# Half-precision softmax split: the low half's subtraction moved from two engines to one

## Chip, cores and metric

One core of one Trainium2 chip runs the whole kernel. The metric is the device time of one execution in microseconds (us). The kernel before takes 1481.31 us, the median of three runs (1479.34 to 1484.07). What a measurement of it can tell from no change is about 0.3%, or 4.4 us.

## What is computed

The reference adds three blocks to an input of 16 sequences x 256 tokens x 128 features:

```
x = x + 0.5 * ffn(layernorm(x))     # soft phase 0
x = x + linear_attention(layernorm(x))
x = x + 0.5 * ffn(layernorm(x))     # soft phase 2
# ffn: h = LN(x); x += softmax_attention(h)   (16 heads of 8, causal)
#      h = LN(x); x += mixture of 8 experts, top 2, silu(h w1) * (h w2) w3
# attention: attn = softmax(mask(q k^T) / sqrt(8)); ctx = attn v; ctx wo + bo
```

The change touches only the softmax attention, which runs twice (phases 0 and 2, "soft"). Both of its runs are called softmax cores here.

## The kernel before

**Batches and groups.** A softmax core goes over B = 16 sequences b, and in each over S = 4 groups g of GH = 4 heads. It runs from about 96 to 425 us and again from about 974 to 1300 us of the span. In front of each stands a stage that makes q, k, v; behind each stands the stage of the experts (39 tiles). The linear attention lies between.

**The probabilities in two halves.** With the causal mask, a group has three blocks of 128 x 128 per head, so a tile of 128 partitions x 3 x 4 x 128 = 1536 columns. ScalarE writes exp() into `pf` in f32 (L613) and casts it into `p_hi` in f16 (L630). Then p_lo = pf - p_hi is taken, also in f16. `pf`, `p_hi` and `p_lo` are double buffered by g % 2. TensorE multiplies p_hi and p_lo with the values (L429, function `values`), and sums both in f32. VectorE subtracts the first two blocks (1024 columns, L933 in `p_low` of the vector block) and GpSimd the third (512 columns, L1315 in `p_low` of the gpsimd block). Each has a semaphore, `p_lo_in` and `p_lo2_in`. Two places wait for both: `values` on TensorE and `exps` on ScalarE, which must not overwrite `pf` of two groups ago.

**VectorE's order** is written out in `iteration` (L1019). In step g of sequence b it does `maxima` of the next group (L920, two of the blocks, then L924, the third, both read PSUM), then something of an earlier sequence, then `p_low` of the group before:

- g = 0: `back_add(b-2)` (L969 to L975), `p_low(b-1, 3)`, `place_of(b-3)` (L1011, L1013)
- g = 1: `x_step(b-2)` (L981, x_all = 0.5 y2 + x_all, two f32 inputs in SBUF), `p_low(b, 0)`
- g = 2: `back_context(b-1)` (L946, L948, L953: cx = num * rden, two f32 inputs in SBUF), `p_low(b, 1)`
- g = 3: `choose(b-2)` (L991 to L1004: top 2 experts; L993 a subtraction of two SBUF inputs, L997 and L998 small casts), `p_low(b, 2)`

**GpSimd's order** is written out in `iteration` (L1319):

- g = 0: `p_low(b-1, 3)`, `back_rstd(b-2)` (L1291 to L1294, waits for VectorE's L975), `scatter(b-4, 3)`
- g = 1: `p_low(b, 0)`, `slots(b-3)` (L1250, three of L1253, L1255, each waiting for the one before), `scatter(b-3, 0)`
- g = 2: `p_low(b, 1)`, `scatter(b-3, 1)`
- g = 3: `p_low(b, 2)`, `scatter(b-3, 2)`

A scatter (L1265) is an indirect DMA that GpSimd issues, 128 rows of the normalized tokens to their expert's place. From sequence 4 on all of this is there ("steady" below); in sequences 0 to 3 the parts of earlier sequences are partly missing. Behind the last sequence the chain of `back_rstd`, `choose`, `slots` and scatters goes on alone (the tail) and ends with the load of the first expert tile.

**TensorE's order** in step g: `natural(g+1)` (scores for the maxima, L379, L383), `turned(g)` (transposed scores with mask and minus the maximum, L403 to L410), `values` of two groups before, and at g = 3 `back_turn(b-1)` (L331, needs cx) and `back_wo(b-1)` (L337, L340). SyncE loads `qst` and `kst` of the next sequence in two halves, each once `turned` has read the old one (L1433).

Of the kernel before, what the change touches and what calls it, by code (L numbers as in the profile page):

```python
# [16 lines left out]
ALU = mybir.AluOpType  # L17
# [3 lines left out]
P = 128  # L21
B = 16
# [5 lines left out]
S = G  # L28
GH = H // G
# [39 lines left out]
def build(nc, x, Wq, Wk, Wv, Wo, ln1_s, ln1_b, wq, wk, wv, wo, bo, ln2_s, ln2_b, gate_w, w1, w2, w3, out):  # L69
    ctx = ExitStack()  # L70

    def sb(name, shape, dt=F32):
        return ctx.enter_context(nc.sbuf_tensor(name, shape, dt))

    with ctx:
# [64 lines left out]
        pf = sb("pf", [P, 2, 3, GH, P])  # L140
        p_hi = sb("p_hi", [P, 2, 3, GH, P], F16)
        p_lo = sb("p_lo", [P, 2, 3, GH, P], F16)
# [16 lines left out]
        def parts_of(ph, g):  # L159

            if ph["soft"] or g < 2:
                return p_hi[:, g % 2, :, :, :], p_lo[:, g % 2, :, :, :]
            return more[:, g - 2, :, :, :], more[:, g, :, :, :]
# [37 lines left out]
        def sem(name):  # L201
            return ctx.enter_context(nc.semaphore(name))

        x_in, w_in, consts, outs, passed = [sem("tokens_in_0"), sem("tokens_in_1")], sem("w_in"), sem("consts"), sem("outs"), sem("passed")
# [7 lines left out]
        shared = sems("all", "xn_in hi_in v_hi ht_in v_done qk_done v_out turn_done cx_in pv_out spread_done act_spread "  # L212
                             "dve_spread turned exped p_hi_in p_lo_in pv_done")
        both = "filled emptied stats rstd cv_back cp_front qk_out "
        of_soft = both + "y_in scored negm_in stats2 rstd2 n2_in cp_back x_in p_lo2_in "
        of_soft += "cv_route cv_place n2_kept top_in chosen_in ranked cp_slot scattered"
        of_linear = both + "neg_in exp_in full_in"
        phases = [dict(shared, n=n, soft=soft, w=0 if soft else 1, back_links=4 if soft else 2,
# [31 lines left out]
        def _(pe):  # L250
# [164 lines left out]
            def values(ph, b, g):  # L415

                pe.wait_ge(ph["v_loaded"][g // 2], ph["n"] * (16 * B) + 16 * (b + 1))
                pe.wait_ge(ph["p_lo_in"], ph["n"] * (S * B) + b * S + g + 1)
                if ph["soft"]:
                    pe.wait_ge(ph["p_lo2_in"], b * S + g + 1)  # L420
                if g % 2 == 0 and not (isinstance(b, int) and b == 0 and g == 0):
                    pe.wait_ge(ph["pv_out"], ph["n"] * (2 * B) + 2 * b + g // 2)
                for j in range(GH):
                    h = GH * g + j
                    for tq, blocks in enumerate((((0, 0),), ((0, 2), (1, 1)))):
                        o = (tq * (H // 2) + h % (H // 2)) * VC
                        todo = [(src, tk, c) for tk, c in blocks for src in parts_of(ph, g)]
                        for i, (src, tk, c) in enumerate(todo):
                            ins = nc.tensor.matmul(bank_pv[:, o:o + VC], src[:, c, j, :],  # L429
                                                   v_hl[:, tk, h, :], start=(i == 0), stop=(i == len(todo) - 1),  # L430
                                                   skip_group_check=True)
                ins.then_inc(ph["pv_done"], 1)
# [122 lines left out]
        def _(sc):  # L555
# [49 lines left out]
            def exps(ph, b, g):  # L605

                sc.wait_ge(ph["turned"], ph["n"] * (S * B) + b * S + g + 1)
                flat = "p a b c -> p (a b c)"
                if ph["soft"]:
                    if not (isinstance(b, int) and b == 0 and g < 2):  # L610
                        sc.wait_ge(ph["p_lo_in"], ph["n"] * (S * B) + b * S + g - 1)
                        sc.wait_ge(ph["p_lo2_in"], b * S + g - 1)
                    nc.scalar.activation(pf[:, g % 2, :, :, :].rearrange(flat),  # L613
                                         banks_t[:, :, :].rearrange("p a b -> p (a b)"), ACT.Exp,
                                         scale=HD ** -0.5).then_inc(ph["exped"], 1)
                else:
                    if not (isinstance(b, int) and b == 0):
                        sc.wait_ge(ph["pv_done"], ph["n"] * (S * B) + b * S + g + 1 - 4)
                    nc.scalar.copy(parts_of(ph, g)[0].rearrange(flat),
                                   (banks_t if g % 2 else banks_n)[:, :, :].rearrange("p a b -> p (a b)"))\  # L620
                        .then_inc(ph["p_hi_in"], 1)
# [155 lines left out]
        def _(ve):  # L777
# [149 lines left out]
            def p_low(ph, b, g):  # L927
                ve.wait_ge(ph["p_hi_in"], ph["n"] * (S * B) + b * S + g + 1)
                flat = "p a b c -> p (a b c)"
                hi, lo = [a.rearrange(flat) for a in parts_of(ph, g)]  # L930
                if ph["soft"]:
                    two = slice(0, 2 * GH * P)
                    nc.vector.tensor_tensor(lo[:, two], pf[:, g % 2, :, :, :].rearrange(flat)[:, two], hi[:, two],  # L933
                                            ALU.subtract)\
                        .then_inc(ph["p_lo_in"], 1)
                else:
                    nc.vector.tensor_tensor(lo, (banks_t if g % 2 else banks_n)[:, :, :].rearrange("p a b -> p (a b)"),  # L937
                                            hi, ALU.subtract)\
                        .then_inc(ph["exped"], 1)
# [241 lines left out]
        def _(gp):  # L1181
            pools = sem("pools")
            c = Chain(gp, pools, 0)
# [124 lines left out]
                select(hi)  # L1308
                select(lo).then_inc(ph["p_lo_in"], 1)

            def p_low(ph, b, g):

                gp.wait_ge(ph["p_hi_in"], ph["n"] * (S * B) + b * S + g + 1)
                flat = "p b c -> p (b c)"
                nc.gpsimd.tensor_tensor(p_lo[:, g % 2, 2, :, :].rearrange(flat), pf[:, g % 2, 2, :, :].rearrange(flat),  # L1315
                                        p_hi[:, g % 2, 2, :, :].rearrange(flat), ALU.subtract)\
                    .then_inc(ph["p_lo2_in"], 1)

            def iteration(ph, b, place=4):  # L1319
                for g in range(S):  # L1320
                    causal(ph, b, g)
                    if ph["soft"] and g:
                        p_low(ph, b, g - 1)
                    elif ph["soft"] and place > 0:
                        p_low(ph, b - 1, S - 1)
                    if ph["soft"] and g == 0 and place > 1:
                        back_rstd(ph, b - 2)
                    if ph["soft"] and g == 1 and place > 2:
                        slots(ph, b - 3)
                    if ph["soft"] and g == 0 and place > 3:  # L1330
                        scatter(ph, b - 4, 3)
                    if ph["soft"] and g and place > 2:
                        scatter(ph, b - 3, g - 1)
# [13 lines left out]
            def attention(ph):  # L1347
                if ph["soft"]:
                    front_rstd(ph, 0)
                    if ph is phases[0]:  # L1350
                        front_constants()
                    front_rstd(ph, 1)
                    front_rstd(ph, 2)
                else:
                    for pair in range(PAIRS):
                        front_rstd(ph, pair)
                if ph is phases[0]:
                    core_constants()
                    split_weights()
                    nc.gpsimd.iota(n2_all[:, :, P], pattern=[[2 * P, NT]], base=0, channel_multiplier=2,  # L1360
                                   allow_small_or_imprecise_dtypes=True)
                    nc.gpsimd.iota(beyond[:, :, :], pattern=[[TS, NTI], [P, 2]], base=2 * CAP, channel_multiplier=1,
                                   allow_small_or_imprecise_dtypes=True)
                    nc.gpsimd.iota(iota_h[:, :], pattern=[[P, 2]], base=0, channel_multiplier=1,
                                   allow_small_or_imprecise_dtypes=True).then_inc(consts, 1)
                    gp.wait_ge(w_in, weights_in)
                if ph["soft"]:
                    for b in range(B):
                        iteration(ph, b, place=b)
                    back_rstd(ph, B - 2)  # L1370
                    scatter(ph, B - 4, 3)
                    p_low(ph, B - 1, S - 1)
                    slots(ph, B - 3)
                    for n in range(4):
                        scatter(ph, B - 3, n)
                    back_rstd(ph, B - 1)
                    slots(ph, B - 2)
                    for n in range(4):
                        scatter(ph, B - 2, n)
                    slots(ph, B - 1)  # L1380
                    for n in range(4):
                        scatter(ph, B - 1, n)
                else:
                    with gp.Fori(0, B) as b:
                        iteration(ph, b)
# [150 lines left out]
```

## Time and profile before

| | |
|---|---|
| median of three runs | 1481.31 us (1479.34 to 1484.07) |
| the profiled execution: own time / span | 1481.91 / 1479.9 us |
| VectorE (DVE) busy | 1181.4 us, 80% |
| TensorE (PE) busy | 1097.4 us, 74% |
| ScalarE (ACT) busy | 857.6 us, 58% |
| GpSimd (POOL) busy | 803.9 us, 54% |
| L933, DVE, 128x1024, x128 | 159.3 us, 1245 ns each |
| L1315, POOL, 128x512, x128 | 169.3 us, 1323 ns each |
| L981, DVE, 128x256, x32 | 44.9 + 8.6 us |
| mean granted TensorE clock | 0.874 |

Busy times are sums of instruction durations, and a duration runs from the start to the end of one instruction as recorded. An instruction that is held up inside (by a resource and not by a semaphore) shows this as a longer duration. Instructions of one engine overlap a little: L933 lasts 1.22 us, and the next one starts 1.13 to 1.14 us behind its start. An idle time in brackets is one ahead of the instruction, with what ended it.

### The profile page before, as it was taken

How to read it: one execution, taken by the hardware profiler on the slowest of the kernel's cores; microseconds unless marked ns; L12 is line 12 of the kernel's file. 1: busy time of each engine (PE TensorE's matmuls, PEld its weight loads, DVE VectorE, ACT ScalarE, POOL GpSimd, SP SyncE). 2: the span in 40 equal slices, each digit the busy share in tenths (PEclk: the TensorE clock that was granted, in tenths of full speed). 3: DMA queues.
4: the chain of work that ended last, by engine and by line, in shares of the span. 5: the costliest groups of instructions: out<-in, count | busy, mean ns of one | idle time of the engine just before them, and what ended most of it. 6: DMA issues, size and time to landing. Idle time of an engine off the chain costs nothing.

```text
span 1479.9 us, 38139 instructions
## 1 busy us (share of the span) xinstructions
PE 1097.4 (74%) x12590; PEld 822.3 (56%) x12716; DVE 1181.4 (80%) x2394; ACT 857.6 (58%) x1263; POOL 803.9 (54%) x934
## 2 busy tenths in 40 slices
PE   5778878887837994677666664988888888639980
PEld 4656766666625663554443443866666666526660
DVE  6867999999956885887778776878999999748885
ACT  3556877777724553446555552767777777625550
POOL 6533666666663665112666664124666667646661
PEclk9999999999958998887666665999999999959995
DMA  8911111111102332110111110001111111013326
GB/s 296 403 28 37 45 45 46 45 46 48 42 24 74 90 90 79 49 40 15 52 52 53 54 47 1 18 18 37 50 50 44 46 47 48 28 47 85 90 73 183
DMA packets 124875, 98.64 MB, mean 67 GB/s; under 512 B 41584, under 2 KB 116848, under 8 KB 124784
## 3 DMA queue, kind: packets, MB, share of 16 engines
q1 hardware_dynamic: 115696, 78.71, 18.1%
q0 software_dynamic: 9088, 18.76, 3.9%
q8 instruction: 52, 0.85, 0.2%
q14 instruction: 39, 0.32, 0.1%
HBM read 24.61 MB, written 40.94 MB: 44 GB/s over the span
## 4 chain that ended last, share of the span: by engine, by line
DVE 37%; PE 20%; issue 20%; ACT 8%; POOL 6%; DMA 4%; SPq 3%; DVEq 1%; ACTq 0%; POOLq 0%
DVE negm L920 5%; DVE p_lo L933 4%; POOL ys L1341 4%; DVE negm L924 3%; PE banks_t L403 3%; PE banks_n L278 3%; PE banks_t L296 2%; DVE p_lo L1132 2%; ACT pf L741 2%; SPq L1433 2%; DVE x_all L882 2%; DVE pf L1139 2%; DMA kst<-k_all 2%; DVE cx L953 2%; PE banks_t L410 2%
## 5 line engine op out<-in xcount | busy, mean ns | idle before, releaser
L1315 POOL TENSOR_TENSOR p_lo<-pf,p_hi 128x512 f16<-128x512 f32 x128 | 169.3, 1323 | 192.7 <-ACT p_hi L630 191.0
L613 ACT ACTIVATE pf<-banks_t 128x1536 f32<-128x1536 f32 x128 | 185.7, 1451 | 119.5 <-PE banks_t L410 112.4
L1341 POOL DMA_INDIRECT ys<-q_all,dest x156 | 151.0, 968 | 116.3 <-ACT q_all L747 91.3
L403 PE MATMUL banks_t<-qst,kst 128*128 128x512 f16 x480 | 192.4, 426 | 3.7 <-ACT pf L613 2.1
L630 ACT CAST p_hi<-pf 128x1536 f16<-128x1536 f32 x128 | 188.7, 1474 | 1.1
L920 DVE TENSOR_REDUCE negm<-banks_n 128x4 f16<-128x1024 f32 x128 | 155.9, 1218 | 30.4 <-PE banks_n L383 22.5
L410 PEld LDWEIGHTS banks_t<-ident,negm 128*128 128x128 f16 x1536 | 123.2, 101 | 82.8 <-issue 12.9
L933 DVE TENSOR_TENSOR p_lo<-pf,p_hi 128x1024 f16<-128x1024 f32 x128 | 159.3, 1245 | 4.3 <-ACT p_hi L630 4.2
L1265 POOL DMA_INDIRECT xs<-n_all,slot x128 | 132.7, 1037 | 47.7 <-issue 30.3
L410 PE MATMUL banks_t<-ident,negm 128*128 128x128 f16 x1536 | 154.3, 225 | 0.4 <-issue 0.4
L383 PE MATMUL banks_n<-kst,qst 128*128 128x128 f16 x1536 | 127.8, 219 | 35.3 <-DMA kst<-k_all 16.5
L429 PE MATMUL bank_pv<-v_hl,p_hi 128*128 128x17 f16 x1920 | 118.8, 172 | 23.2 <-POOL p_lo L1301 17.9
L429 PEld LDWEIGHTS bank_pv<-v_hl,p_hi 128*128 128x128 f16 x1920 | 110.9, 98 | 41.7 <-issue 41.6
L383 PEld LDWEIGHTS banks_n<-kst,qst 128*128 128x128 f16 x1536 | 107.3, 98 | 30.8 <-issue 0.3
L429 PE MATMUL bank_pv<-v_hl,p_lo 128*128 128x17 f16 x1920 | 117.5, 172 | 0.0
L429 PEld LDWEIGHTS bank_pv<-v_hl,p_lo 128*128 128x128 f16 x1920 | 106.7, 98 | 4.2 <-issue 4.2
L407 PE MATMUL banks_t<-maskt,identb 128*128 128x512 bf16 x254 | 99.8, 393 | 0.0
L1301 POOL TENSOR_SCALAR_AFFINE_SELECT pf<-pf 128x1024 f16<-128x1024 f16 x64 | 68.3, 1091 | 55.0 <-DVE pf L937 55.0
L508 PE MATMUL banks_n<-p_hi,w 128*128 128x256 f16 x472 | 94.6, 281 | 3.0 <-DVE p_lo L1125 2.9
L924 DVE TENSOR_REDUCE negm<-banks_n 128x4 f16<-128x512 f32 x128 | 86.8, 678 | 0.0
L735 ACT CAST p_hi<-pf 128x256 f16<-128x256 f32 x78 | 31.6, 405 | 90.2 <-DVE pf L1139 90.2
L331 PE MATMUL bank_mx<-ident,cx 128*128 128x128 f32 x96 | 27.5, 380 | 68.0 <-DVE cx L953 66.1
(201 smaller groups left out, 3072.9 us busy)
## 6 DMA issues: line engine op xcount, KB each, us to landing
xs<-qst SPq DMA_DIRECT2D x20, 975.0 KB, 25.7
qst<-q_all SPq DMA_DIRECT2D x384, 32.0 KB
kst<-k_all SPq DMA_DIRECT2D x96, 128.0 KB
q_all<-xs SPq DMA_DIRECT2D x78, 130.0 KB
pf<-ys SPq DMA_DIRECT2D x32, 256.0 KB, 3.0
v_hl<-v_all SPq DMA_DIRECT2D x96, 68.0 KB, 2.1
ys<-q_all,dest POOLq DMA_INDIRECT x156
n_all<-L_ffn_w SPq DMA_DIRECT2D x4, 512.0 KB, 7.5
```

Of the source, the lines that this page charges most:

```text
L383: ins = nc.tensor.matmul(banks_n[:, c, j * P:(j + 1) * P], qst[:, g, j, tq * P:(tq + 1) * P], kst[:, g, tk * P:(tk + 1) * P], start=(c == ...
L403: ins = nc.tensor.matmul(banks[:, c, :], kst[:, g, tk * P:(tk + 1) * P], qst[:, g, :, tq * P:(tq + 1) * P], start=True, stop=not ph["soft" ...
L410: ins = nc.tensor.matmul(banks_t[:, c, j * P:(j + 1) * P], negm[:, g % 2, tq, j:j + 1].to_broadcast([P, P]), ident16[:, :], start=False, s ...
L429: ins = nc.tensor.matmul(bank_pv[:, o:o + VC], src[:, c, j, :], v_hl[:, tk, h, :], start=(i == 0), stop=(i == len(todo) - 1), skip_group_c ...
L613: nc.scalar.activation(pf[:, g % 2, :, :, :].rearrange(flat), banks_t[:, :, :].rearrange("p a b -> p (a b)"), ACT.Exp, scale=HD ** -0.5).t ...
L630: nc.scalar.copy(p_hi[:, g % 2, :, :, :].rearrange(flat), pf[:, g % 2, :, :, :].rearrange(flat))\
L920: nc.vector.tensor_reduce(negm[:, g % 2, 1, :], banks_n[:, 1:3, :].rearrange("p c (h k) -> p h c k", h=GH), AX.XY, ALU.max, negate=True).t ...
L924: nc.vector.tensor_reduce(negm[:, g % 2, 0, :], banks_n[:, 0, :].rearrange("p (h k) -> p h k", h=GH), AX.X, ALU.max, negate=True).then_inc ...
L933: nc.vector.tensor_tensor(lo[:, two], pf[:, g % 2, :, :, :].rearrange(flat)[:, two], hi[:, two], ALU.subtract)\
L1265: nc.gpsimd.indirect_dma_start(xs, bass.IndirectOffsetOnAxis(ap=slot[:, T * b + t, k:k + 1], axis=0), n2_all[:, T * b + t, :], None).then_ ...
L1315: nc.gpsimd.tensor_tensor(p_lo[:, g % 2, 2, :, :].rearrange(flat), pf[:, g % 2, 2, :, :].rearrange(flat), p_hi[:, g % 2, 2, :, :].rearrang ...
L1341: nc.gpsimd.indirect_dma_start(ys, bass.IndirectOffsetOnAxis(ap=dest[:, t % YB, h:h + 1], axis=0), y_out[:, t % YB, h, :], None).then_inc( ...
```

## The change

VectorE's subtraction takes the whole tile of 1536 columns. GpSimd's `p_low`, its calls and the semaphore `p_lo2_in` with its waits are removed. Nothing else is changed; the linear phase already subtracts 1536 columns at once on VectorE (L937).

```diff
-        of_soft = both + "y_in scored negm_in stats2 rstd2 n2_in cp_back x_in p_lo2_in "
+        of_soft = both + "y_in scored negm_in stats2 rstd2 n2_in cp_back x_in "
...
                 pe.wait_ge(ph["p_lo_in"], ph["n"] * (S * B) + b * S + g + 1)
-                if ph["soft"]:
-                    pe.wait_ge(ph["p_lo2_in"], b * S + g + 1)
...
                         sc.wait_ge(ph["p_lo_in"], ph["n"] * (S * B) + b * S + g - 1)
-                        sc.wait_ge(ph["p_lo2_in"], b * S + g - 1)
...
                 if ph["soft"]:
-                    two = slice(0, 2 * GH * P)
-                    nc.vector.tensor_tensor(lo[:, two], pf[:, g % 2, :, :, :].rearrange(flat)[:, two], hi[:, two],
-                                            ALU.subtract)\
+                    nc.vector.tensor_tensor(lo, pf[:, g % 2, :, :, :].rearrange(flat), hi, ALU.subtract)\
                         .then_inc(ph["p_lo_in"], 1)
...
-            def p_low(ph, b, g):
-
-                gp.wait_ge(ph["p_hi_in"], ph["n"] * (S * B) + b * S + g + 1)
-                flat = "p b c -> p (b c)"
-                nc.gpsimd.tensor_tensor(p_lo[:, g % 2, 2, :, :].rearrange(flat), pf[:, g % 2, 2, :, :].rearrange(flat),
-                                        p_hi[:, g % 2, 2, :, :].rearrange(flat), ALU.subtract)\
-                    .then_inc(ph["p_lo2_in"], 1)
-
             def iteration(ph, b, place=4):
                 for g in range(S):
                     causal(ph, b, g)
-                    if ph["soft"] and g:
-                        p_low(ph, b, g - 1)
-                    elif ph["soft"] and place > 0:
-                        p_low(ph, b - 1, S - 1)
...
                     scatter(ph, B - 4, 3)
-                    p_low(ph, B - 1, S - 1)
                     slots(ph, B - 3)
```

## Rows read from the trace of the kernel before

**Rows 1.** The waits of VectorE from 180 to 400 us.

```profile
DVE negm L920 <- DVE base L1013: 3.6, 11, 0.3
```

**Rows 2.** The chain that ended last, 104 to 122 us: start, duration, what.

```profile
107.85 3.05 DMA kst<-k_all
```

**Rows 3.** VectorE's groups by form, whole span: busy, mean ns | idle.

```profile
L933 DVE TENSOR_TENSOR p_lo<-pf,p_hi 128x1024 f16<-128x1024 f32 x128 | 159.3, 1245 | 4.3 <-ACT p_hi L630 4.2
...
L1132 DVE TENSOR_TENSOR p_lo<-pf,p_hi 128x512 f16<-128x512 f32 x78 | 53.2, 682 | 0.0
...
L937 DVE TENSOR_TENSOR p_lo<-banks_t,p_hi 128x1536 f16<-128x1536 f32 x16 | 28.0, 1751 | 1.7 <-ACT p_hi L619 1.5
```

**Rows 4.** VectorE's timeline in a steady sequence.

```profile
251.68 0.17 DVE L997 CAST n_all<-topi 128x2 uint32 x1 [0.25 <-DVE topi L995]
...
260.34 2.12 DVE L981 SCALAR_TENSOR_TENSOR x_all<-y,x_all 128x256 f32 x1
262.38 1.27 DVE L933 TENSOR_TENSOR p_lo<-pf,p_hi 128x1024 f16<-128x1024 f32 x1
...
266.13 1.47 DVE L953 TENSOR_TENSOR cx<-num,rden 128x256 f32<-128x256 f32 x1
```

**Rows 5.** GpSimd's timeline in the same sequence.

```profile
251.29 0.99 POOL L1265 DMA_INDIRECT xs<-n_all,slot  x1 [0.16 <-issue]
...
259.89 1.07 POOL L1265 DMA_INDIRECT xs<-n_all,slot  x1 [0.56 <-issue]
260.99 1.17 POOL L1315 TENSOR_TENSOR p_lo<-pf,p_hi 128x512 f16<-128x512 f32 x1
262.10 0.45 POOL L1250 TENSOR_TENSOR at_slot<-onehot,pos 128x32 f32<-128x32 f32 x1
262.64 1.65 POOL L1253 TENSOR_TENSOR at_slot<-at_slot 128x16 f32<-128x16 f32 x3
...
266.15 1.16 POOL L1315 TENSOR_TENSOR p_lo<-pf,p_hi 128x512 f16<-128x512 f32 x1
```

**Rows 6.** VectorE's timeline in one uncommon sequence, 1213 to 1224 us.

```profile
1213.66 0.42 DVE L981 SCALAR_TENSOR_TENSOR x_all<-y,x_all 128x256 f32 x1
...
1218.07 0.42 DVE L953 TENSOR_TENSOR cx<-num,rden 128x256 f32<-128x256 f32 x1
...
1223.20 1.92 DVE L997 CAST n_all<-topi 128x2 uint32 x1 [0.15 <-DVE topi L995]
```

**Rows 7.** GpSimd's timeline in the same sequence.

```profile
1222.90 0.98 POOL L1265 DMA_INDIRECT xs<-n_all,slot  x1 [0.17 <-issue]
1223.91 1.17 POOL L1315 TENSOR_TENSOR p_lo<-pf,p_hi 128x512 f16<-128x512 f32 x1
```

**Rows 8.** VectorE's groups by form, 157 to 407 us.

```profile
L933 DVE TENSOR_TENSOR p_lo<-pf,p_hi 128x1024 f16<-128x1024 f32 x50 | 62.5, 1250 | 0.0
L981 DVE SCALAR_TENSOR_TENSOR x_all<-y,x_all 128x256 f32 x11 | 23.3, 2117 | 0.0
...
L993 DVE TENSOR_TENSOR prob<-top 128x2 f32 x11 | 5.9, 539 | 1.8 <-DVE top L991 1.8
```

**Rows 9.** The same, 1044 to 1280 us.

```profile
L933 DVE TENSOR_TENSOR p_lo<-pf,p_hi 128x1024 f16<-128x1024 f32 x47 | 58.7, 1250 | 0.0
...
L953 DVE TENSOR_TENSOR cx<-num,rden 128x256 f32<-128x256 f32 x12 | 16.6, 1384 | 0.4
L993 DVE TENSOR_TENSOR prob<-top 128x2 f32 x11 | 4.9, 446 | 3.2 <-DVE top L991 3.2
```

**Rows 10.** GpSimd's line 1250, whole span: shortest, median, longest ns.

```profile
L1250 POOL TENSOR_TENSOR at_slot<-onehot,pos x32: 250/448/457, 160.9 to 1310.9; 128x32 f32<-128x32 f32 x32
```

**Rows 11.** VectorE's timeline where the tail begins.

```profile
414.95 0.42 DVE L969 TENSOR_TENSOR y<-bank_mx,yb 128x256 f32<-128x256 f32 x1 [2.51 <-PE bank_mx L340]
...
417.27 1.22 DVE L933 TENSOR_TENSOR p_lo<-pf,p_hi 128x1024 f16<-128x1024 f32 x1
```

**Rows 12.** GpSimd's timeline at the same place.

```profile
417.41 1.67 POOL L1293 TENSOR_TENSOR rs<-rs,half 128x2 f32<-128x2 f32 x1
```

## The prediction

> **What bounds the kernel now.** I read the busy slices first: VectorE is the busiest engine, and in the softmax cores it is busy in nearly every slice. Then its waits in the steady part: the longest one on anything is a gap of 0.3 us behind its own L1013 [rows 1], and none is on another engine. So from about 157 to 407 us, and from 1044 to 1280 us, every microsecond that VectorE's instructions gain or lose goes to the end. Last I read the chain that ended last at the two ends of a core. In sequences 0 to 3 it runs through the loads of `kst` (3.05 us for one landing) and TensorE [rows 2]; VectorE idles there. In the tail it runs through GpSimd's small operations and scatters. The stages outside the softmax cores are not touched.
>
> **The cost.** A subtraction of 512 columns takes 0.682 us, one of 1536 takes 1.751 us [rows 3], so 1024 more columns cost 1.069 us and 512 more 0.535 us. An undisturbed L933 of 1024 columns is then 0.682 + 0.535 = 1.217 us. The 1536 columns that L937 subtracts have one input in PSUM, and here both are in SBUF. The 512 columns of L1132 have both in SBUF and lie on the same line, so I take no difference. L933 runs 50 times in the first steady stretch and 47 times in the second [rows 8, 9]: 97 x 0.535 = 51.9 us. The other 31 of 128 lie in sequences 0 to 3, where the idle time ahead of L920 takes up 0.5 us per step while TensorE and the loads of `kst` lead [rows 2], and next to the tail, where VectorE then waits 2.51 us for TensorE [rows 11]. I cost these at nothing. If that cover were gone they would cost at most 31 x 0.535 = 16.6 us, and I keep 3 us of it for the range. One late subtraction per core is on the chain in another way: L1293 on GpSimd stands inside L933 and ends 0.59 us behind it (419.08 against 418.49) [rows 11, 12]. It ends 0.535 us later: 1.1 us for both cores. Cost: **53.0 us**.
>
> **What goes away.** GpSimd's L1315 is not on VectorE's queue and no wait of VectorE names it. Yet it holds VectorE up. L953 starts at 266.13 us, L1315 at 266.15 and ends at 267.31, and L953 ends only at 267.60, after 1.47 us [rows 4, 5]; without GpSimd beside it, it takes 0.42 us [rows 6]. L981 takes 2.12 us and ends 0.30 us behind L1315; alone it takes 0.42 us [rows 4 to 6]. So an instruction of VectorE with two inputs in SBUF stands still until GpSimd's subtraction is over. Term by term:
>
> - **L953.** Slowed by 1.05 us in 12 + 11 sequences; the second group shows it as 16.6 us for 12, of which one is free, (16.6 - 12 x 0.42) = 11.6 = 11 x 1.05 [rows 9]. Behind the change only scatters lie beside it, and beside a scatter alone a VectorE instruction runs freely: L997 takes 0.17 us at 251.68, inside the scatter at 251.29 [rows 4, 5]. Gain 23 x 1.05 = **24.2 us**.
> - **L981.** In 12 + 11 sequences 2.12 us. It starts 0.45 us into a scatter (259.89 to 260.96), and L1315 starts only behind that. Still L981 does not get through. L997 at 1223.20 shows the same: 0.30 us into a scatter, with L1315 next, it lasts 1.92 us up to L1315's end [rows 6, 7], while L997 at 251.68, with no subtraction ready behind the scatter, does not. I conclude that a GpSimd operation that is ready behind a scatter holds VectorE up already during the scatter. After the change the one behind it is L1250, ready too. Both chains start at the end of the same L933, so the 0.45 us stays. L1250 takes 0.25 us when nothing holds it [rows 10]. L981 ends at 1.10 us (scatter and gap) + 0.25 + 0.28 = 1.63 us from the scatter's start, so it lasts 1.18 us. Gain 23 x (2.12 - 1.18) = **21.6 us**.
> - **L993 and L997.** L993 lasts 5.9 + 4.9 us in 22 cases [rows 8, 9], against about 0.17 for so small an operation: gain 10.8 - 3.7 = 7.1 us; and one L997 of 1.92 us [rows 6] gives 1.75. **8.8 us**.
> - **L933 itself.** 62.5 + 58.7 - 97 x 1.217 = 3.1 us above free. Of that 0.05 us per sequence comes from L1250, as in 262.38 [rows 4], and stays: gain **2.0 us**.
>
> Against this stand two small terms. In the uncommon sequence L981 is free today (0.42 us at 1213.66) [rows 6], since GpSimd was late; it will be 1.18: +0.8 us. And the first L1253, which now waits behind L933 [rows 5], may come in ahead of it: 0.1 us x 23 = +2.3 us.
>
> GpSimd itself loses 1.2 us four times per sequence and just idles more; its scatters of a sequence then run one after the other, with nothing queued behind them. ScalarE and TensorE wait for p_lo of a group one step later than it is made, so 0.5 us more is covered.
>
> **The sum.** 53.0 + 0.8 + 2.3 - 24.2 - 21.6 - 8.8 - 2.0 = -0.5 us. The first L953 of the tail also releases TensorE's L331 1.05 us earlier, which is among the 23. Against the profiled execution's own 1481.9 us this gives 1481.4; the median of the runs shown is 0.6 us lower, so I say **1481 us**: no change that can be measured, 4.4 us being the bound. The change takes a hold-up of 57 us off VectorE and puts 53 us of arithmetic in its place.
>
> By the Trainium skill ("SBUF — State Buffer", Reading the diagram under SBUF: two separate sides) the pair of interfaces that VectorE shares with GpSimd is an exclusive lock, taken for the whole instruction by whichever starts first, and a VectorE operation with two SBUF inputs meets it only against a GpSimd operation that reads SBUF. Taken at its word, L981, which starts ahead of L1315, should not be held up today, and the trace does not agree: 2.12 us. For L953 against scatters it agrees.
>
> **Rivals.**
>
> - **L981 becomes free.** It starts 0.6 us ahead of L1250. For it: L1250 is a different, small operation, and the hold-up during a scatter is shown for L1315 alone. Against it: nothing in the order or the waits sets L1250 apart. Price: 23 x (1.18 - 0.42) = 17.5 us less, plus the 0.8: 1463 us, faster. This is also what the skill's rule of the first to start would give.
> - **The slot chain holds the interface.** L1250 and the three L1253 (about 0.2 us each and 0.07 between) now come straight behind the scatter, and VectorE might get no turn among them. L981 would then last 1.18 + 3 x 0.27 = 2.0 us: +18.6 us, less the 2.3 for L1253: 1481.4 + 16.3, about 1497 us, slower. Against it: today L1250 lasts 0.45 and not 0.25 us because L981 gets its turn between L1315 and it. It decides from where L981 lasts on average over about 1.4 us.
> - **L1315 was hidden and its removal gives nothing**, so that only the arithmetic counts: 1481 + 53 = 1534 us. The rows of L953 and L981 speak too clearly against it; 1 in 100.
>
> **Chances.** No measurable change 0.44: the forecast with its own spread. Faster 0.36: 0.22 for a free L981, and 0.14 for more of the small terms than I counted (casts and L946 held up less, TensorE released 1 us earlier at each L331). Slower 0.20: 0.10 for the slot chain, 0.10 for early sequences that cover less (up to 3 us of 16.6) with a larger L1253 term. The range goes from a free L981 to half way to the slot chain: **1461 to 1491 us**.
>
> **What will show it.** L933 at 1.75 us, 128 times, 68 us more busy. L953 at 0.42 in steady sequences. L993 at 0.16 to 0.17. L981: 1.18 (forecast), 0.42 (faster) or 2.0 us (slower). The length of a steady sequence, now about 20.1 to 20.3 us from one L981 to its next, within 0.3 us of that. L1293 in the tail at 2.2 us. VectorE's waits in the steady stretch still on itself alone; if L920 waits for TensorE there, the bound has moved and the sum is wrong. If L953 stays over 1 us beside scatters, the scatters hold VectorE up, and up to 24 us come back.

## The result and the profile after

The changed kernel takes 1461.8 us against 1482.7 us (medians of four runs each), a ratio of 0.986 with a 95% interval of 0.982 to 0.989: 1.4% faster. It lies in the predicted range (1461 to 1491), 0.8 us above its lower end, but the forecast itself was 1481 us, no change; what came is the first rival, to which the prediction gave 0.22.

The page of the changed kernel first: span, engines, and the groups of the subtraction and of the scatters.

```profile
span 1463.3 us, 38014 instructions
...
PE 1102.0 (75%) x12716; PEld 819.0 (56%) x12716; DVE 1169.8 (80%) x2394; ACT 857.3 (59%) x1263; POOL 686.4 (47%) x806
...
L929 DVE TENSOR_TENSOR p_lo<-pf,p_hi 128x1536 f16<-128x1536 f32 x128 | 223.9, 1749 | 3.8 <-ACT p_hi L627 3.7
...
L1260 POOL DMA_INDIRECT xs<-n_all,slot x128 | 164.5, 1285 | 55.4 <-issue 37.6
```

VectorE does 64.6 us more subtraction (159.3 to 223.9) and is nevertheless 11.6 us less busy. The groups by form show where the 76 us between these two went:

```profile
L948 DVE TENSOR_TENSOR cx<-num,rden 128x256 f32<-128x256 f32 x48 | 27.9, 582 | 1.7
...
L976 DVE SCALAR_TENSOR_TENSOR x_all<-y,x_all 128x256 f32 x22 | 9.6, 435 | 0.0
L976 DVE SCALAR_TENSOR_TENSOR x_all<-y,x_all 128x256 f32<-128x256 f32 x10 | 4.4, 442 | 1.0 <-DVE base L1008 1.0
...
L988 DVE TENSOR_TENSOR prob<-top 128x2 f32 x22 | 3.6, 163 | 4.9 <-DVE top L986 4.9
```

L976 is the old L981: 53.5 us before, 14.0 now. L948 is the old L953, 52.9 us before (the linear phase included), 27.9 now. L988 is the old L993 [rows 8, 9]. The timelines of a steady sequence put it side by side with [rows 4, 5], VectorE first:

```profile
258.83 1.75 DVE L929 TENSOR_TENSOR p_lo<-pf,p_hi 128x1536 f16<-128x1536 f32 x1
...
262.94 0.43 DVE L976 SCALAR_TENSOR_TENSOR x_all<-y,x_all 128x256 f32 x1
263.30 1.75 DVE L929 TENSOR_TENSOR p_lo<-pf,p_hi 128x1536 f16<-128x1536 f32 x1
...
267.53 0.42 DVE L948 TENSOR_TENSOR cx<-num,rden 128x256 f32<-128x256 f32 x1
```

and GpSimd:

```profile
262.49 1.07 POOL L1260 DMA_INDIRECT xs<-n_all,slot  x1 [0.56 <-issue]
263.59 1.55 POOL L1245 TENSOR_TENSOR at_slot<-onehot,pos 128x32 f32<-128x32 f32 x1
265.23 0.78 POOL L1248 TENSOR_TENSOR at_slot<-at_slot 128x16 f32<-128x16 f32 x3
...
268.32 2.14 POOL L1260 DMA_INDIRECT xs<-n_all,slot  x1 [0.30 <-issue]
```

L976 starts 0.45 us into the scatter, exactly as before, but now lasts 0.43 us. GpSimd is the one that waits: L1245 (the old L1250) starts inside L929, lasts 1.55 us and ends 0.09 us behind it, and a scatter that starts inside L929 takes 2.14 us. GpSimd has the time. VectorE's waits from 180 to 390 us (who waited, for whom: in total, times, longest) are on VectorE's own instructions alone; the longest in total, twin of [rows 1]:

```profile
DVE negm L917 <- DVE base L1008: 3.7, 11, 0.3
```

Sequence for sequence, from one set of L967 (the old L972) to the same 11 sequences later, the first steady stretch takes 210.8 us instead of 222.2 (about 19.14 us each), the second 212.2 instead of 220.8. The rest of the cores, up to their last L967, gives 1.4 and 2.1 us. That is 23.5 us. Of it the profiled execution gives 6.9 back where nothing was changed: 1.9 ahead of the first core, 1.1 net over the parts between and behind, and 3.9 in the early sequences of both cores (4.5 lost in the first, 0.6 gained in the second). Most of it begins with one landing of `kst`, here before and after:

```profile
128.15 2.10 DMA kst<-k_all
```

```profile
129.79 3.97 DMA kst<-k_all
```

The landing gives 1.9 us. Behind it TensorE ran at a granted clock of 0.50, the lower of its two levels, where it had 1.00 before, and the matmuls from the landing to the end of the transposed scores took 6.1 us instead of 3.3. The stretch at half clock (span; busy PE, PEld, DVE, ACT, POOL; granted clock, DMA share, GB/s):

```profile
133.76:139.54 5.78, 5.73 (x32) 3.74 (x33) 2.99 (x3) 1.74 (x2) 0.00 (x0) 0.50 0.00 0
```

From the first subtraction to the first L967 of the core this execution takes 37.9 us, the kernel before 33.5, and seven later kernels with the same early work or more on it 31.6 to 33.8. So it is this execution's, not the change's.

### The profile page after: what moved, and what is told of

It is laid out like the page before. It is cut to its first block, busy times and chain, and to the rows that moved or that the text cites. A ratio compares the mean times of both kernels' runs of the same rounds, so it can differ in the third digit from the quotient of the medians.

```text
span 1463.3 us, 38014 instructions
## 1 busy us (share of the span) xinstructions
PE 1102.0 (75%) x12716; PEld 819.0 (56%) x12716; DVE 1169.8 (80%) x2394; ACT 857.3 (59%) x1263; POOL 686.4 (47%) x806
## 4 chain that ended last, share of the span: by engine, by line
DVE 32%; issue 21%; PE 21%; ACT 10%; POOL 6%; DMA 5%; SPq 3%; DVEq 1%; ACTq 1%; POOLq 0%
DVE negm L917 6%; POOL ys L1324 4%; PE banks_n L278 3%; PE banks_t L296 3%; PE banks_t L403 3%; DMA kst<-k_all 2%; SPq L1415 2%; DVE p_lo L1127 2%; ACT pf L738 2%; DVE negm L921 2%; DVE x_all L879 2%; DVE pf L1134 2%; PE banks_n L383 2%; PE banks_n L379 2%; ACT p_hi L616 2%
## 5 line engine op out<-in xcount | busy, mean ns | idle before, releaser
L929 DVE TENSOR_TENSOR p_lo<-pf,p_hi 128x1536 f16<-128x1536 f32 x128 | 223.9, 1749 | 3.8 <-ACT p_hi L627 3.7
L1286 POOL TENSOR_SCALAR rs<-mv 128x2 f32<-128x2 f32 x32 | 44.3, 1385 | 343.0 <-DVE mv L970 285.2
L1260 POOL DMA_INDIRECT xs<-n_all,slot x128 | 164.5, 1285 | 55.4 <-issue 37.6
L403 PE MATMUL banks_t<-qst,kst 128*128 128x512 f16 x480 | 186.2, 413 | 4.4 <-DVE pf L932 2.2
L410 PEld LDWEIGHTS banks_t<-ident,negm 128*128 128x128 f16 x1536 | 119.6, 99 | 77.7 <-issue 3.8
L410 PE MATMUL banks_t<-ident,negm 128*128 128x128 f16 x1536 | 150.1, 221 | 0.0
L427 PE MATMUL bank_pv<-v_hl,p_hi 128*128 128x17 f16 x1920 | 118.8, 172 | 19.9 <-POOL p_lo L1296 17.9
L383 PEld LDWEIGHTS banks_n<-kst,qst 128*128 128x128 f16 x1536 | 108.9, 99 | 31.6 <-issue 1.7
L379 PE MATMUL banks_n<-maskb,identb 128*128 128x512 bf16 x256 | 98.8, 386 | 36.7 <-DVE negm L917 19.1
L732 ACT CAST p_hi<-pf 128x256 f16<-128x256 f32 x78 | 31.6, 405 | 90.9 <-DVE pf L1134 90.9
```

What stands on the lines that cost most here:

```text
L379: nc.tensor.matmul(banks_n[:, 1 - part, :], identb[:, :], mask, start=True, stop=False, skip_group_check=True)
L383: ins = nc.tensor.matmul(banks_n[:, c, j * P:(j + 1) * P], qst[:, g, j, tq * P:(tq + 1) * P], kst[:, g, tk * P:(tk + 1) * P], start=(c == ...
L403: ins = nc.tensor.matmul(banks[:, c, :], kst[:, g, tk * P:(tk + 1) * P], qst[:, g, :, tq * P:(tq + 1) * P], start=True, stop=not ph["soft" ...
L410: ins = nc.tensor.matmul(banks_t[:, c, j * P:(j + 1) * P], negm[:, g % 2, tq, j:j + 1].to_broadcast([P, P]), ident16[:, :], start=False, s ...
L929: nc.vector.tensor_tensor(lo, pf[:, g % 2, :, :, :].rearrange(flat), hi, ALU.subtract)\
L1260: nc.gpsimd.indirect_dma_start(xs, bass.IndirectOffsetOnAxis(ap=slot[:, T * b + t, k:k + 1], axis=0), n2_all[:, T * b + t, :], None).then_ ...
```

## Experiments

**The arithmetic alone, and the hold-up alone.** The first kernel leaves the third block's subtraction out:

```diff
+                    nc.vector.memset(lo_flat, 0.0)
                     ve.wait_ge(x_in[0], 16)
...
-                    nc.vector.tensor_tensor(lo, pf[:, g % 2, :, :, :].rearrange(flat), hi, ALU.subtract)\
+                    two = slice(0, 2 * GH * P)
+                    nc.vector.tensor_tensor(lo[:, two], pf[:, g % 2, :, :, :].rearrange(flat)[:, two], hi[:, two],
+                                            ALU.subtract)\
```

> The changed kernel, but VectorE subtracts only the first 1024 columns and nobody subtracts the third block: its low half stays what it was (it is set to zero once ahead of the tokens' arrival), so this kernel leaves that part of the computation out. It shows the price of the arithmetic alone. My theory (VectorE is the bound, 97 subtractions on its path at 0.535 us each, and 1.1 us in the tails): 53 us less than the changed kernel's 1461.8, so about 1409 us, and 73 us less than the kernel before, which is the whole hold-up by GpSimd's subtraction. Rival (part of the arithmetic is covered, and the gain of the change came from somewhere else): 1425 us or more.

Measured: 1434.2 us, 0.966 of the kernel before (0.964 to 0.968). That is 29 us below the changed kernel by the two ratios, not 53, and in the rival's range (1425 or more): the first half of the rival is true, part of the arithmetic is covered. A sequence takes 17.9 us instead of 19.14, so only 1.24 of the 2.14 us come off. VectorE's waits from 180 to 390 us say why:

```profile
DVE negm L918 <- PE banks_n L383: 7.2, 11, 0.7
DVE negm L918 <- DVE base L1011: 3.6, 11, 0.3
```

With less to do VectorE waits for TensorE's scores in each sequence. So there is a second bound at 17.9 us. The changed kernel lies above it, and there the 2.14 us of a sequence count in full. The other half of the rival, that the gain came from somewhere else, is what the next kernel decides.

The second kernel does both subtractions, GpSimd's into a spare tile `scr`:

```diff
+        scr = sb("scr", [P, 2, GH * P], F16)
...
+                nc.gpsimd.tensor_tensor(scr[:, g % 2, 0:COLS], pf[:, g % 2, 2, :, :].rearrange(flat)[:, 0:COLS],
+                                        p_hi[:, g % 2, 2, :, :].rearrange(flat)[:, 0:COLS], ALU.subtract)\
+                    .then_inc(ph["p_lo2_in"], 1)
```

> The changed kernel plus GpSimd's old subtraction at its four old places, with its semaphore and ScalarE's wait, but written to a spare tile that nobody reads: VectorE has the 1536 columns and GpSimd its 512 at the same time. My theory (the gain came from taking GpSimd's reads out of VectorE's way, 57 to 74 us): 53 us more than the kernel before, about 1535 us, L976 (the old L981) back at about 2.1 us and L948 (the old L953) back at 1.4 to 1.5 us. Rival (what was gained lies in the waits for the second semaphore on TensorE and ScalarE): with VectorE's own work unchanged and only ScalarE's wait back, within 10 us of 1462.

Measured: 1533.6 us (forecast about 1535), 1.032 (1.030 to 1.034), that is 47 us above the kernel before (forecast 53). The groups:

```profile
L953 DVE TENSOR_TENSOR cx<-num,rden 128x256 f32<-128x256 f32 x48 | 56.5, 1178 | 1.7
L981 DVE SCALAR_TENSOR_TENSOR x_all<-y,x_all 128x256 f32 x22 | 45.0, 2043 | 0.0
...
L993 DVE TENSOR_TENSOR prob<-top 128x2 f32 x22 | 4.5, 206 | 4.9 <-DVE top L991 4.9
```

The hold-ups are back, inside the instructions, with GpSimd's operation. TensorE does not wait for the second semaphore here, so that wait is not their cause. ScalarE's wait is back together with the operation; two kernels further down have it too, without the hold-up of L981 (0.43 us with the operation behind the slots, 0.42 us in the last kernel), so it is not the cause either. The 6 us that are missing to 53 us are about what L993 gives: 4.5 us against 10.8 in the kernel before, since it mostly no longer meets the subtraction.

**Where the split costs nothing.** In the next two kernels GpSimd takes the third block of some groups only (SPLIT is (3,), then (2, 3)):

```diff
+                    cols = slice(0, (2 if g in SPLIT else 3) * GH * P)
+                    nc.vector.tensor_tensor(lo[:, cols], pf[:, g % 2, :, :, :].rearrange(flat)[:, cols], hi[:, cols],
+                                            ALU.subtract)\
```

> The changed kernel, but for group 3 of each sequence GpSimd subtracts the third block again, at its old place in step g = 0, where VectorE at that moment does maxima and an addition that read PSUM. Groups 0 to 2 stay on VectorE alone. My theory (GpSimd's subtraction costs only where it meets an instruction of VectorE with two SBUF inputs): one L929 of four is 0.535 us shorter and nothing is held up, 24 x 0.535 = 13 us less than the changed kernel: about 1449 us. Rival (any GpSimd subtraction costs VectorE as much as it saves): 1460 us or more.

> As the kernel with group 3 split, and group 2 is split too, whose GpSimd subtraction stands in step g = 3 next to VectorE's choose. My theory: another 0.535 us per sequence saved, less the hold-up of L988 (the old L993), 0.17 to 0.5 us: 2 to 9 us less than with group 3 alone, 1440 to 1447 us. Rival (the held-up small instructions cost as much as is saved): the same time as with group 3 alone, or more.

Measured: 1446.2 us (forecast about 1449), 0.974 (0.971 to 0.977), and 1448.4 us (forecast 1440 to 1447), 0.974 (0.971 to 0.977). A sequence takes 18.60 us with group 3 split, 0.54 less than 19.14, as forecast to the hundredth. With group 2 split as well it takes 18.70 us. There the rival was right:

```profile
L996 DVE TENSOR_TENSOR prob<-top 128x2 f32 x22 | 17.0, 774 | 4.9 <-DVE top L994 4.9
```

L996 (the old L993) is held up for 0.61 us (0.77 against 0.16), more than the 0.17 to 0.5 of the forecast and more than the 0.54 that the shorter subtraction gives.

**Why L981 was held up before GpSimd's operation began.** One GpSimd subtraction per sequence, for group 0, into the spare tile, and ScalarE waits for it. It stands ahead of the slots (the edit is the one with `scr` above, with SPLIT = (0,)), with COLS = 512, 256, 128 and 32; once with one input; once behind the slots. Each of these six kernels ran once; what is read from them are durations that come back in 23 sequences of that execution.

> The changed kernel plus one GpSimd subtraction of 512 columns per sequence, for group 0 at its old place in step g = 1, behind the scatter and ahead of the slots, written to a spare tile that nobody reads. L976 (the old L981) starts 0.45 us into the scatter. If what is ready behind a scatter can hold VectorE up already during the scatter: L976 at 2.1 us, L948 (the old L953) stays at 0.42, a sequence 1.7 us longer than the changed kernel's 19.14 us. If L981 was held up by something else (the other three subtractions, or the second semaphore on TensorE): L976 at 0.43 us.

> The same with 32 columns in place of 512, as many as L1250 has (the old L1250, the one that stands behind the scatter in the changed kernel and did not hold L976 up). If the number of columns decides, that is, only a long operation takes hold ahead of its start: L976 at 0.43 us. If any operation of this kind, ready behind a scatter, holds VectorE up, and L1250 is an exception for another reason: L976 at about 1.2 us (0.65 to the scatter's end, 0.25 for the operation, 0.28 of its own).

> The changed kernel plus one GpSimd subtraction per sequence ahead of the slots in step g = 1, now of 256 columns (512 columns held L981 for 2.12 us, 32 columns not at all). If the hold-up ahead of the operation's start is the operation being long enough, and 256 are enough: L981 at 0.65 + about 0.6 + 0.28 = 1.5 us. If the threshold lies above: L981 at 0.43 us and the subtraction waits behind L934, as with 32 columns.

> The same with 128 columns: L981 at 0.65 + about 0.4 + 0.28 = 1.3 us if 128 are enough, 0.43 us if not.

> As with 512 columns for group 0 ahead of the slots, but the operation has one input (p_hi times 1, f16 to f16) and not two. If it is GpSimd's reading of SBUF that counts, however many inputs: L976 held up until this operation ends, 0.65 + its own duration + 0.28 us. If it takes two inputs on GpSimd's side: L976 at 0.43 us.

> The same as with 512 columns for group 0, but placed behind the slots and ahead of the scatter in step g = 1. Then L1250's successor stands behind the scatter as in the changed kernel, so L976 at 0.43 us by every theory, and the subtraction meets L941 and L948 (the old L946 and L953) instead: together 0.8 to 1.2 us longer, if an instruction with two SBUF inputs that starts inside GpSimd's subtraction waits for its end. If only L976 is prone to it: nothing, 19.14 us per sequence.

| GpSimd's operation behind the scatter | L981, steady | sequence | the one run |
|---|---|---|---|
| L1250 alone (changed kernel) | 0.43 us | 19.14 us | |
| 32 columns | 0.42 | 19.19 | 1463.2 us |
| 128 columns | 0.62 | 19.37 | 1468.1 |
| 256 columns | 0.85 | 20.03 | 1478.8 |
| 512 columns | 2.12 | 20.88 | 1495.4 |
| 512 columns, one f16 input | 0.81 | 19.97 | 1476.6 |
| (behind the scatter: L1250) 512 columns behind the slots | 0.43 | 19.7 to 20.5 | 1487.8 |

In all of them L981 starts 0.45 us into the scatter. With 512 and with 32 columns the forecast came true. With 256 and 128 columns and with one input neither number did (1.5 or 0.43, 1.3 or 0.43, and the whole operation or 0.43 us): from 128 to 512 columns the hold-up grows step by step and does not set in at full. The rows of L981 with 512 columns, with 32 and with 128:

```profile
238.17 2.12 DVE L981 SCALAR_TENSOR_TENSOR x_all<-y,x_all 128x256 f32 x1
```

```profile
239.99 0.42 DVE L981 SCALAR_TENSOR_TENSOR x_all<-y,x_all 128x256 f32 x1
```

```profile
240.81 0.62 DVE L981 SCALAR_TENSOR_TENSOR x_all<-y,x_all 128x256 f32 x1
```

and GpSimd with 128 columns:

```profile
240.36 1.08 POOL L1265 DMA_INDIRECT xs<-n_all,slot  x1 [0.56 <-issue]
241.47 1.97 POOL L1317 TENSOR_TENSOR scr<-pf,p_hi 128x128 f16<-128x128 f32 x1
```

Here L981 ends (241.43) before the subtraction starts (241.47), and is still 0.20 us longer than alone. So it is held up during the scatter, by an operation that has not started by its record, and the more so the more columns that one has: 0, 0.20 and 0.43 us with 32, 128 and 256 columns. With 256 and 512 columns L981 ends inside the operation's record, but undisturbed it would have been over 0.87 us behind the scatter's start, 0.24 us ahead of the operation's. With 512 it does not end until 0.29 us behind the operation. The runs show this dependence on size, not what GpSimd does with the operation ahead of its record.

The hold-up does not last through the whole scatter. In the kernel before, L946, which reads two inputs in SBUF as well, stands in a scatter with L1315 and its 512 columns behind it in 23 sequences, 0.22 us behind the scatter's start, and takes 0.41 us, as if alone. ScalarE had written L1315's input `p_hi` by 264.26 us, before the scatter began. VectorE, GpSimd and ScalarE, in the sequence of [rows 4, 5]:

```profile
265.30 0.41 DVE L946 TENSOR_TENSOR num<-pv_sb 128x256 f32<-128x256 f32 x1
```

```profile
265.08 1.04 POOL L1265 DMA_INDIRECT xs<-n_all,slot  x1 [0.54 <-POOL slot L1255]
```

```profile
262.80 1.46 ACT L630 CAST p_hi<-pf 128x1536 f16<-128x1536 f32 x1
```

L946 is over 0.63 us into the scatter, L981 undisturbed would be at 0.87. So if both scatters are alike, what holds L981 up acts only behind the first 0.63 us of one. One case does not fit: L997 of the uncommon sequence, a cast with one input, would have been over 0.47 us into its scatter and was held [rows 6]. No run moves the start of one instruction through the scatter, so when the hold-up begins stays open.

With 256 columns part of the loss (20.03 against 19.14) is in L934 behind L981, 2.22 us instead of 1.75, since it meets the subtraction itself. The one-input case behaves like 256 columns of two inputs, not like 512 (0.81 us, and 2.20 for L934), so neither two inputs nor f32 are needed on GpSimd's side. Both read 512 elements per partition; that these decide and not the columns fits the table but was not tested by itself. Behind the slots the subtraction meets L946 instead, which starts inside it, and L953 comes behind it (0.42 us): 0.55 us longer, not the 0.8 to 1.2 of the forecast. What a sequence takes above 19.7 us there is VectorE waiting for TensorE's scores, up to 0.7 us. VectorE, then GpSimd:

```profile
244.68 0.96 DVE L946 TENSOR_TENSOR num<-pv_sb 128x256 f32<-128x256 f32 x1
```

```profile
241.58 1.55 POOL L1250 TENSOR_TENSOR at_slot<-onehot,pos 128x32 f32<-128x32 f32 x1
...
244.21 1.16 POOL L1317 TENSOR_TENSOR scr<-pf,p_hi 128x512 f16<-128x512 f32 x1
```

**A version below both kernels.** All four groups are split again, but for groups 0 to 2 GpSimd waits until VectorE's own subtraction is done, so that it runs during the maxima, which read PSUM:

```diff
-                gp.wait_ge(ph["p_hi_in"], ph["n"] * (S * B) + b * S + g + 1)
+                gp.wait_ge(ph["p_hi_in" if g == S - 1 else "p_lo_in"], ph["n"] * (S * B) + b * S + g + 1)
```

> The split of the kernel before for all four groups (VectorE 1024 columns, GpSimd 512), but for groups 0 to 2 GpSimd waits for VectorE's own subtraction of the same group (p_lo_in) and not for p_hi; for group 3 it waits for p_hi as before. GpSimd's 1.16 us then run while VectorE does the two maxima (1.74 us), which read PSUM alone. If the hold-up is only a matter of which instructions meet: nothing is held up, VectorE needs 19.14 - 4 x 0.535 = 17.0 us per sequence, the other chain that bounded the kernel with 1024 columns takes over at 17.9 us, and the kernel comes to 1430 to 1440 us, below both kernels. If GpSimd's small operations, pushed back by this, now meet L946, L953 and L981: 18.5 us or more per sequence, 1445 us or more.

Measured: 1434.3 us (forecast 1430 to 1440), 0.968 (0.965 to 0.971), 3.2% below the kernel before, and with the whole computation. Its groups and one of its waits from 180 to 380 us:

```profile
L936 DVE TENSOR_TENSOR p_lo<-pf,p_hi 128x1024 f16<-128x1024 f32 x128 | 157.3, 1229 | 6.3 <-ACT p_hi L633 6.2
...
L1320 POOL TENSOR_TENSOR p_lo<-pf,p_hi 128x512 f16<-128x512 f32 x128 | 150.3, 1174 | 208.6 <-DVE p_lo L936 201.7 <-ACT p_hi L633 5.3
...
L984 DVE SCALAR_TENSOR_TENSOR x_all<-y,x_all 128x256 f32 x22 | 9.1, 416 | 0.0
```

```profile
DVE negm L923 <- PE banks_n L385: 5.8, 12, 0.5
```

GpSimd still does its 128 subtractions, and L984 (the old L981) takes 0.42 us; all waits for the second semaphore, on TensorE and on ScalarE, are in place. So it is a matter of what the subtraction meets. A sequence takes 17.7 to 18.1 us, the bound found with 1024 columns alone, and the intervals of the two ratios overlap (0.966 and 0.968). The chain that ended last runs, from 200 to 350 us, through the loads and TensorE:

```profile
by line: issue 22.5%; SPq L1438 16.3%; DMA kst<-k_all 12.4%; PE banks_t L412 7.8%; PE banks_t L405 7.3%; PE banks_t L409 4.9%; ACT n L662 4.7%; PE banks_n L385 4.4%; ACT yb L654 4.4%; ACT pf L616 3.9%; PE bank_mx L333 2.6%; PE bank_mx L350 
```

## Why the prediction was right and wrong

- **The time**: the forecast was 1481 us, -0.5 us; measured are -20.9. That 1461.8 still lies in the range is owed to the lower end, which was set at the first rival, and not to the sum.
- **The bound**: right. VectorE bounds both kernels in the steady stretches; its waits of the changed kernel are on itself. That another bound lies at 17.9 us a sequence I had not seen; it does not touch the sum but it does what lies below.
- **The cost, 53.0 us**: right. L929 takes 1.749 us (forecast 1.751), both inputs in SBUF or not. The early sequences covered theirs, and L1293 (now L1288) in the tail came to 2.20 us, as forecast:

```profile
410.42 2.20 POOL L1288 TENSOR_TENSOR rs<-rs,half 128x2 f32<-128x2 f32 x1
```

- **L953, 24.2 us**, and **L993 with L997, 8.8 us**: right. L948 takes 0.42 us in every steady sequence beside scatters, L988 0.16. The row on which this leaned was weak, L997 being a cast with one input; L946, undisturbed in a scatter with two, would have been the better one.
- **L981, 21.6 us**: this is the step that failed. That an operation ready behind a scatter can hold L981 up during the scatter was right, since 512 columns bring back 2.12 us. But I took it to hold for any operation, L1250 with its 32 columns too. It depends on the size, and 32 columns cost nothing. The term is 23 x 1.70 = 39.1 us instead of 21.6. I also overlooked L946, which 512 columns behind a scatter left alone 23 times: already the kernel before showed that "ready behind a scatter" is not enough. The reason against the rival, that "nothing in the order or the waits sets L1250 apart", was true and not enough: its size did, and stood in the row.
- **L1253 ahead of L933, +2.3 us, the uncommon sequence, +0.8, and 1.1 of L933's own 3.1 us kept**: none of it came. GpSimd is the one that waits now, and L929 is undisturbed at 1.749 us on average.
- **The sum** with these replaced is 53.0 - 24.2 - 39.1 - 8.8 - 3.1 = -22.2 us, against 23.5 measured in the cores and 20.9 between the medians. More came off than that where the tail begins: the last step but one of each core is 1.9 and 2.6 us shorter, a steady sequence about 1.0. See below.
- The Trainium skill's rule ("SBUF — State Buffer", SBUF: two separate sides) that the first to start takes the interface gave the right time here: L976 starts ahead of L1245 and is free. But L981 started 0.66 us ahead of the subtraction of 128 columns and was held up all the same. With the starts that the record shows, the trace does not bear the rule out there.

## What to carry to other kernels

When VectorE is the bound, look at the longest against the shortest duration of its operations that read SBUF, those with two inputs above all: here the difference (2.12 against 0.42, 1.47 against 0.42, 0.99 against 0.16 us) was time lost to GpSimd that no wait shows. The cast L997 with one input lost time too, once (1.92 against 0.17). Before work is moved off GpSimd, try to move it in time: let it wait for the VectorE instruction that reads SBUF, so that it runs beside those that read PSUM; here that gave 3.2% and the move 1.4%. And weigh a small operation by its size, not by its place in the queue alone.

## What was not expected

- A scatter is held up too: mostly 2.14 us when it starts inside L929 (27 of 128 do), 0.95 to 1.24 us otherwise. In the kernel before only 3 started inside L933.
- A granted clock that was not in the sum: at the last L953 but one of the first core TensorE stood idle for 2.72 us before and then ran at half clock. Now it idles 1.80 us at the same place and runs at full clock. The stretches, before and after (span; busy PE, PEld, DVE, ACT, POOL; granted clock, DMA share, GB/s):

```profile
408.70:415.00 6.30, 6.08 (x58) 4.68 (x60) 3.56 (x14) 3.90 (x5) 3.98 (x3) 0.55 0.04 13
```

```profile
402.00:408.30 6.30, 4.15 (x59) 3.27 (x58) 4.85 (x14) 5.71 (x10) 3.11 (x2) 1.00 0.11 34
```

  The chain from `back_turn` to `back_wo` was on the path there and took 6.2 us (408.70 to 414.9). Now it takes 3.7 (404.06 to 407.8), and the path runs beside it, through `p_hi` and L929; VectorE's addition starts 3.9 us behind `back_turn`, not 6.2. That the shorter idle time kept the clock up is not shown: in the kernel before, the same matmul stood behind 1.57 us of idle time with a granted clock of 0.50 at 227.1 us and of 1.00 at 207.0.
- Why 512 columns hold VectorE up to the end of the operation and 256 for 0.43 us only stays open; sizes between, and other operations than a subtraction or a scaling, were not tried.
